# Where an output bias is added and which engine writes the normalised rows, in a two-layer attention and expert kernel

## The chip, the cores and the metric

The kernel runs on one core of a Trainium2 chip. A core has a matrix engine (TensorE, PE in the profile, with its weight loads as PEld), a vector engine (VectorE, DVE), an engine for functions of one operand (ScalarE, ACT), GpSimd (POOL), and SyncE (SP), which here issues nearly all transfers. Each takes its own instructions in order and waits for the others at semaphores. The metric is the time of one execution on the device, in microseconds (us), as the median of several runs.

## The reference

Four batches of 512 rows with 256 features pass through two layers, each an attention block and an expert block. Cut to its spine:

```python
# _layernorm(x) = (x - mean) / sqrt(var + 1e-5), row by row, without gain or shift
x = x + L0_xattn(_layernorm(x), ctx, ctx, mask)          # 16 heads, out @ Wo.T          (no output bias)
x = L0_ffn(_layernorm(x)):
    attn = attention(src) @ Wo + bo                      # src = _layernorm(x)
    y = _layer_norm(src + attn, ln1_g, ln1_b)            # with gain and shift
    y + one of 4 experts, chosen per row; _layer_norm(.., ln2_g, ln2_b)   # the result is added to x
x = x + L1_xattn(_layernorm(x), ctx, ctx, 2 * fside)     # attention(..) @ Wo.T + bo
x = x + L1_ffn(_layernorm(x))                            # 2 of 16 experts per row and 2 shared ones
```

Three attention blocks end in an output projection, two of them with a bias `bo`, and after each sum the rows are normalised for the next block. The bias, the residual and the projection are only added together, so the bias may be added to the residual at any time before.

## The kernel before, in words

All 2048 rows live in on-chip memory as 16 tiles of 128 rows by 256 features: `x` is the residual stream, `Z` the normalised rows. The program is a sequence of blocks, and all engines meet at a barrier between two blocks. Nothing is scheduled by a program: in each block every engine's instructions stand in the order in which the code of its `@block` function issues them, and a wait holds all that follows on that engine. The blocks that matter here:

- `output` (L927), called three times, for the output stages. Four rounds, one for each batch (b = 0 to 3). TensorE transposes the attention's result (L953) one round ahead of its use, ScalarE copies the turned tiles out of PSUM into `oT` (L983), TensorE multiplies them by `wo` (L967), four row tiles a round, with four PSUM tiles `py` in rotation. VectorE adds each product to the residual (L1030), takes the statistics of the row (L1001, L1038, L1040); ScalarE takes the square root (L976, one instruction of 128x4 for a round), VectorE the reciprocal (L1006), and VectorE writes the four normalised tiles (L1011; in the second call, with gain and shift, two instructions a tile, L1017 and L1021). The last three belong to `scale(b)`, which for rounds 0 to 2 stands behind the second add of the next round. Where there is a bias (second and third call) VectorE starts with four adds of 128x1024 (L995).
- ScalarE's order in `output` before: the copies of rounds 0, 1 and 2, the square root of round 0, the copies of round 3, the square roots of rounds 1 to 3. TensorE waits for both copies of a round before the matmuls of that round.
- `attention_direct` (L749), the attention of the second block, just ahead of the second output stage. VectorE takes the row minima of the scores (L897, four a head) and every fourth head divides a group of results by its sums (L520, L522).
- `queries` (L1404), ahead of the third attention. It adds the experts' output to `x` (L1539), normalises (L1542 to L1554), turns and projects the queries, and splits them into two parts: `hi` (ScalarE, L1507) and `lo` (VectorE, L1532, function `rest`). SyncE issues 2 MB of `y`, 1 MB of `common`, four transfers of 1 MB of the side input (L1436) and then the first keys (L497, L499). When the last `lo` is done GpSimd subtracts the first tile of the side input (L1464), and that ends the block.
- `attention_turned` (L525), third attention: GpSimd prepares one 128x2048 tile for each of 64 heads (L630), from a ring of four tiles that SyncE refills with 1 MB each (L588). At the 32nd head `fetch` loads `wo` and `bo` (L298, L300).

Of the kernel before, what the change touches and what calls it, by code (L numbers as in the profile page):

```python
# [19 lines left out]
ACT = mybir.ActivationFunctionType  # L20
AX = mybir.AxisListType.X

P = 128
B, S, D, H = 4, 512, 256, 16
DK = D // H
# [70 lines left out]
class Program:  # L96
# [652 lines left out]
    def attention_direct(self, QS, KS, O, fetch, ring, XS, s_qk):  # L749
# [4 lines left out]
        with ExitStack() as ctx:  # L754
# [33 lines left out]
            with nc.Block() as block:  # L788
# [99 lines left out]
                def _(eng):  # L888
                    eng.memset(pO[:], 0.0).then_inc(s_pad, 1)  # L889
                    for i in range(LAST):  # L890
# [3 lines left out]
                        for c in range(ST):  # L894
# [32 lines left out]
    def output(self, O, biased, base, dst, z, affine=None, fetch=None):  # L927


        nc, w, brow = self.nc, self.wo, self.bo  # L930
        with ExitStack() as ctx:
# [3 lines left out]
            rs = self.sb("rs", [P, NT], ctx=ctx)  # L935
            bank = self.ps("tp", [P, 4, 512], ctx)
            py = self.ps("py", [P, 4, 512], ctx)
            names = ("s_tr", "s_ev", "s_y", "s_a", "s_b", "s_st", "s_ag", "s_var", "s_dev", "s_rs", "s_g")
            s_tr, s_ev, s_y, s_a, s_b, s_st, s_ag, s_var, s_dev, s_rs, s_g = (self.sem(n, ctx) for n in names)
            with nc.Block() as block:  # L940
# [6 lines left out]
                def _(eng):  # L947
# [10 lines left out]
                    eng.wait_ge(self.s_wo, 32 if biased else 16)  # L958
# [13 lines left out]
                def _(eng):  # L972
# [4 lines left out]

                    for b in range(B):
# [5 lines left out]
                        if b >= 2:  # L984
                            deviations(b - 2)
                    deviations(B - 2)
                    deviations(B - 1)

                @block.vector
                def _(eng):  # L990
                    if biased:
                        eng.wait_ge(self.s_wo, 32)
                        for b in range(B):
                            rows = slice(b * ST, (b + 1) * ST)
                            eng.tensor_tensor(dst[:, rows, :], base[:, rows, :], brow[:].unsqueeze(1).to_broadcast([P, ST, D]),  # L995
                                              ALU.add).then_inc(s_b, 1)
                    src = dst if biased else base

# [4 lines left out]
                    def scale(b):  # L1003
# [1316 lines left out]
```

## Time and profile before

| | |
|---|---|
| three runs | 1748.32, 1748.68 and 1756.85 us, median 1748.68 us |
| the profiled execution | 1752.8 us, of it 1751.0 us span |
| busy, share of the span | PE 88%, DVE 63%, ACT 46%, POOL 26% |
| first output stage | 355 to 379 us of the span |
| `attention_direct`, second output stage | 438 to 666 us, 666 to 698 us |
| `queries`, third attention | 898 to 939 us, 939 to 1248 us |
| third output stage | 1249 to 1273 us |

An instruction is named by its line in the code, its engine and what it writes from what. A time in square brackets behind a row of the timeline is how long the engine sat idle before it and whom it waited for. TensorE's clock is given as a share of its full 2.4 GHz: 1.00 or 0.50. The chain of waits that the page prints covers only the last blocks, since every block ends in a barrier; so for each block the question is what ends it.

### The profile page before, as it was taken

To read this page: it belongs to the slowest core of one execution; us is meant where nothing else is said; L and a number is where in the kernel's file an instruction comes from. 1 tells how busy PE (TensorE), PEld (TensorE's weight loads), DVE (VectorE), ACT (ScalarE), POOL (GpSimd) and SP (SyncE) were. 2 spreads that over 40 slices of the span, in tenths; PEclk is the share of its full clock that TensorE was granted. 3 is DMA by queue.
4 is the path that set the end of the run, shared out by engine and by line. 5 is a ranking of instruction groups with operands and counts; after the bars stand their busy time and mean duration, and the time that the engine had idled before them with its cause. 6 is when DMAs were issued, how large, how long until landed. Compare 5 with 4: busy or idle time off the path is not lost. (4 is left out here: it accounts for less than half of the span.)

```text
span 1751.0 us, 24325 instructions
## 1 busy us (share of the span) xinstructions
PE 1543.9 (88%) x8312; PEld 1024.6 (59%) x8312; DVE 1108.5 (63%) x2778; ACT 812.9 (46%) x1301; POOL 455.2 (26%) x249
## 2 busy tenths in 40 slices
PE   6799999978999996699956899889888998999992
PEld 3566666655644444489944555555654556677772
DVE  6699999856887767446566888788733530122223
ACT  1388888721566672322217787777422121211110
POOL 0000000012000000301116999999122143111111
PEclk9899999999999999889978999999979999999997
DMA  7745653106343314557746988988060012144434
GB/s 252 258 153 158 180 140 85 49 13 216 92 111 104 104 43 151 198 197 248 250 183 220 313 297 300 294 290 283 4 217 0 0 49 79 56 155 157 150 111 159
DMA packets 142088, 276.68 MB, mean 158 GB/s; under 512 B 25616, under 2 KB 70160, under 8 KB 132624
## 3 DMA queue, kind: packets, MB, share of 16 engines
q1 hardware_dynamic: 134720, 258.99, 45.3%
q0 software_dynamic: 5136, 14.06, 2.2%
q10 hardware_dynamic: 2112, 2.10, 0.4%
q8 instruction: 68, 1.11, 0.3%
q14 instruction: 52, 0.43, 0.1%
HBM read 215.37 MB, written 59.69 MB: 157 GB/s over the span
## 5 line engine op out<-in xcount | busy, mean ns | idle before, releaser
L703 DVE CUSTOM_DVE_ANT_0 X<-pS,M 128x512 f32<-128x512 f32 x512 | 340.5, 689 | 54.6 <-POOL M L630 38.8
L653 PE MATMUL pT<-ident,X 128*128 128x128 f32 x2048 | 305.5, 272 | 1.7 <-ACT PT L739 1.7
L644 PE MATMUL pS<-k,q 65*128 65x512 f32 (+1 forms) x512 | 253.9, 496 | 55.0 <-DVE mx L703 35.9
L630 POOL TENSOR_TENSOR M<-C,M 128x2048 f32<-128x2048 f32 x63 | 286.0, 4603 | 6.9 <-DMA M<-in_fside_Bx16xSxS 6.5
L653 PEld LDWEIGHTS pT<-ident,X 128*128 128x128 f32 x2048 | 254.0, 140 | 41.6 <-issue 4.2
L510 PE MATMUL pO<-PT,V 128*17 128x512 f32 x1536 | 200.6, 598 | 1.0 <-ACT OT L924 1.0
L644 PEld LDWEIGHTS pS<-k,q 65*128 65x128 f32 (+1 forms) x512 | 97.9, 191 | 174.3 <-DVE mx L703 104.4
L897 DVE TENSOR_REDUCE nm<-pS 128x1 fp32r<-128x512 f32 x256 | 163.5, 684 | 40.0 <-PE pS L839 29.1
L731 ACT ACTIVATE X<-X,nm 128x512 f32<-128x512 f32 x256 | 164.0, 712 | 27.9 <-DVE nm L709 27.9
L731 ACT ACTIVATE X<-X,mx 128x512 f32<-128x512 f32 x256 | 165.2, 715 | 3.6 <-DVE mx L703 3.3
L716 DVE COPY PT<-pT 128x1024 f32<-128x1024 f32 x128 | 156.0, 1219 | 6.4 <-PE pT L653 6.4
L2040 PE MATMUL p<-xT,w 128*128 128x320 f32 x512 | 145.3, 437 | 0.5 <-ACT xT L2100 0.5
L739 ACT COPY PT<-pT 128x1024 f32<-128x1024 f32 x128 | 128.1, 1000 | 35.0 <-PE pT L653 34.0
L2126 DVE TENSOR_TENSOR g<-act,p 128x320 f32<-128x320 f32 x64 | 31.2, 487 | 166.0 <-ACT act L2089 166.0
L839 PE MATMUL pS<-rk,rq 65*128 65x512 f32 x256 | 116.4, 455 | 6.7 <-DVE pO L889 6.0
L1905 PE MATMUL p<-zT,w 128*128 128x512 f32 x256 | 122.2, 623 | 0.0
L2040 PEld LDWEIGHTS p<-xT,w 128*128 128x128 f32 x512 | 95.4, 190 | 40.4 <-issue 2.7
L2089 ACT ACTIVATE act<-p 128x320 f32<-128x320 f32 x64 | 28.0, 437 | 180.1 <-PE p L2040 180.1
L849 PE MATMUL pT<-rq,rk 97*128 97x512 f32 x256 | 102.2, 410 | 0.8 <-ACT PT L916 0.8
L839 PEld LDWEIGHTS pS<-rk,rq 65*128 65x128 f32 x256 | 48.9, 191 | 70.7 <-DVE nm L897 37.1
L916 ACT ACTIVATE PT<-pT 128x1024 f32<-128x1024 f32 x64 | 65.5, 1024 | 44.7 <-PE pT L849 44.4
L2106 POOL DMA_INDIRECT top_out<-ys,xs x32 | 30.5, 955 | 213.2 <-DVE ys L2140 211.7
(303 smaller groups left out, 2119.0 us busy)
## 6 DMA issues: line engine op xcount, KB each, us to landing
M<-in_fside_Bx16xSxS SPq DMA_DIRECT2D x64, 1024.0 KB, 7.3
w<-in_L_ffn_ew SPq DMA_DIRECT2D x48, 512.0 KB, 5.8
w<-in_L_ffn_W SPq DMA_DIRECT2D x23, 1024.0 KB, 5.4
q<-q_stacks SPq DMA_DIRECT2D x192, 64.0 KB, 3.8
M<-mask SPq DMA_DIRECT2D x16, 512.0 KB, 3.8
k<-k_stacks SPq DMA_DIRECT2D x128, 64.0 KB, 3.1
xs<-top_in SPq DMA_DIRECT2D x51, 128.5 KB, 2.2
k_stacks<-hi SPq DMA_DIRECT2D x24, 256.0 KB, 2.6
```

The lines of the kernel that those rows point to most:

```text
L510: ins = eng.matmul(pO[j * STRIP:j * STRIP + DK + 1, cols], V[:, g * GROUP + j, kt, :], PT[:, g % 2, j, kt, cols], start=(kt == 0 and cols. ...
L630: eng.tensor_tensor(M[:, slot], C[:, b % 2], M[:, slot], ALU.subtract).then_inc(s_m, 1)
L644: eng.matmul(pS[:, qt % 2, :], of, by, start=True, stop=True).then_inc(s_s, 1)
L653: ins = eng.transpose(pT[:, kt, qt * P:(qt + 1) * P], X[:, t % 3, qt, kt * P:(kt + 1) * P], self.ident[:])
L703: eng.tensor_tensor_reduce(X[:, i % 3, qt, :], pS[:, qt % 2, :], M[:, slot, qt, :], 2.0 if mask is None else 1.0, HIGHEST if mask is None ...
L716: eng.tensor_copy(PT[:, g % 2, j, 2:4, :], pT[:, 2:4, :]).then_inc(s_ed, 1)
L731: eng.activation(X[:, h % 3, qt, :], X[:, h % 3, qt, :], ACT.Exp, bias=(nm if mask is not None else mx)[:, h % 3, qt:qt + 1], scale=1.0 if ...
L739: eng.copy(PT[:, g % 2, j, 0:2, :], pT[:, 0:2, :]).then_inc(s_ea, 1)
L839: eng.matmul(bank("scores", i, qt), q[0:AUX + 1, slot, j, qt * P:(qt + 1) * P], k[0:AUX + 1, slot, j, :], start=True, stop=True).then_inc( ...
L897: eng.tensor_reduce(nm[:, pair % 2, j * ST + c:j * ST + c + 1], bank("scores", i, c), AX, ALU.min).then_inc(s_x, 1)
L1905: ins = eng.matmul(bank[:, q % 2, :], w[:, k, m * P:(m + 1) * P], zT[:, k, c * S:(c + 1) * S], start=(k == 0), stop=(k == KD - 1))
L2040: ins = eng.matmul(bank[:, m % 2, 0:CAP], w[:, i % 4, k, m * P:(m + 1) * P], xT[:, i % 2, k, :], start=(k == 0), stop=(k == KD - 1))
```

## The change

It does three things.

1. In the first and third output stage (those without gain and shift) the normalised rows are written as `x * rs + off`, with `off = -mean * rs`. VectorE computes `off` with a new instruction of 128x4 for each round, and ScalarE writes the tiles with `Identity`, with `off` as bias and `rs` as scale, both read from memory for each partition. Of the last round VectorE still writes two tiles. ScalarE now does this in `normal(b - 1)`, behind the copies of round b.
2. The bias of the second output stage is added to `Z` in `attention_direct`, one tile of 128x256 behind every third head (16 in all). The bias of the third is added to `x` in `queries`, 128x1024 for each batch, behind the first `lo` of that batch.
3. `wo` and `bo` of the third attention are loaded in `queries`, between the side input and the keys, and no longer at the 32nd head.

```diff
@@ attention_direct, VectorE, end of each of its steps
+                        n, at = divmod(i - 12, 3)
+                        if at == 0 and 0 <= n < NT:
+                            if n == 0:
+                                eng.wait_ge(self.s_wo, 32)
+                            eng.tensor_tensor(x[:, n, :], x[:, n, :], self.bo[:], ALU.add)
@@ output, ScalarE
+                    def normal(b):
+                        deviations(b)
+                        if affine is not None:
+                            return
+                        eng.wait_ge(s_off, b + 1)
+                        eng.wait_ge(s_tr, (b + 1) * KD)
+                        for n in range(b * ST, (b + 1) * ST - (2 if b == B - 1 else 0)):
+                            eng.activation(z[:, n, :], dst[:, n, :], ACT.Identity, bias=off[:, n:n + 1], scale=rs[:, n:n + 1])
+
                     for b in range(B):
                         for k in range(KD):
                             n = b * KD + k
                             eng.wait_ge(s_tr, n + 1)
                             need(eng, s_y, (b - 1) * ST)
                             eng.copy(OT[:, b % 2, k, :], bank[:, n % 4, :]).then_inc(s_ev, 1)
-                        if b >= 2:
-                            deviations(b - 2)
-                    deviations(B - 2)
-                    deviations(B - 1)
+                        if b >= 1:
+                            normal(b - 1)
+                    normal(B - 1)
@@ output, VectorE
-                    if biased:
-                        eng.wait_ge(self.s_wo, 32)
-                        for b in range(B):
-                            rows = slice(b * ST, (b + 1) * ST)
-                            eng.tensor_tensor(dst[:, rows, :], base[:, rows, :], brow[:].unsqueeze(1).to_broadcast([P, ST, D]),
-                                              ALU.add).then_inc(s_b, 1)
@@ output, VectorE, scale(b), behind the reciprocal
+                        if affine is None:
+                            eng.scalar_tensor_tensor(out=off[:, b * ST:(b + 1) * ST], in0=mv[:, b * ST:(b + 1) * ST, 0], scalar=-1.0,
+                                                     in1=rs[:, b * ST:(b + 1) * ST], op0=ALU.mult, op1=ALU.mult).then_inc(s_off, 1)
+                            if b == B - 1:
+                                eng.wait_ge(s_tr, (b + 1) * KD)
+                                for n in rows[-2:]:
+                                    eng.tensor_scalar(z[:, n, :], dst[:, n, :], mv[:, n, 0:1], rs[:, n:n + 1], ALU.subtract, ALU.mult)
+                            return
                         eng.wait_ge(s_tr, (b + 1) * KD)
-                        if affine is None:
-                            for n in rows:
-                                eng.tensor_scalar(z[:, n, :], dst[:, n, :], mv[:, n, 0:1], rs[:, n:n + 1], ALU.subtract, ALU.mult)
-                            return
@@ queries, SyncE
+                    self.load_out(eng, wo, bo)
                     for pair in range(2):
                         self.load_two_keys(eng, KS, self.k2, pair, pair, self.s_qk[pair])
@@ queries, VectorE, rest(b)
+                            if m == 0:
+                                rows = slice(b * ST, (b + 1) * ST)
+                                eng.wait_ge(s_z, (b + 1) * ST)
+                                eng.wait_ge(self.s_wo, 32)
+                                eng.tensor_tensor(x[:, rows, :], x[:, rows, :], self.bo[:].unsqueeze(1).to_broadcast([P, ST, D]), ALU.add)
```

On ScalarE, in the first output stage, the order is this before (`oT` are the turned tiles, `rs` the deviations, `Z` the normalised rows):

```order
 L745 COPY OT<-pO 128x512 x2
 L567 UNCONDITIONAL_BRANCH
-L971 UNCONDITIONAL_BRANCH
-L983 COPY oT<-tp 128x512 x6
-L976 ACT_TABLE_LOAD
-L976 ACTIVATE rs<-rs 128x4
-L983 COPY oT<-tp 128x512 x2
-L976 ACTIVATE rs<-rs 128x4 x3
-L940 UNCONDITIONAL_BRANCH
```

and this with the change:

```order
+L977 UNCONDITIONAL_BRANCH
+L998 COPY oT<-tp 128x512 x4
+L982 ACT_TABLE_LOAD
+L982 ACTIVATE rs<-rs 128x4
+L991 ACTIVATE Z<-x,off,rs 128x256 x4
+L998 COPY oT<-tp 128x512 x2
+L982 ACTIVATE rs<-rs 128x4
+L991 ACTIVATE Z<-x,off,rs 128x256 x4
+L998 COPY oT<-tp 128x512 x2
+L982 ACTIVATE rs<-rs 128x4
+L991 ACTIVATE Z<-x,off,rs 128x256 x4
```

The copies of round 2 now stand behind the deviations and the four tiles of round 0, those of round 3 behind the ones of round 1.

On VectorE, at the end of `queries`, before and then with the change (`lo` is the second part of a query tile, `x` by `bo` the moved bias):

```order
L1547 TENSOR_SCALAR rs<-mv 128x4
L1532 TENSOR_TENSOR lo<-whole,hi 128x512 x2
L1551 RECIPROCAL rs<-rs 128x4
L1554 TENSOR_SCALAR Z<-x,mv,rs 128x256 x4
L1532 TENSOR_TENSOR lo<-whole,hi 128x512 x6
```

```order
L1561 TENSOR_SCALAR rs<-mv 128x4
L1541 TENSOR_TENSOR lo<-whole,hi 128x512
L1546 TENSOR_TENSOR x<-x,bo 128x1024
L1541 TENSOR_TENSOR lo<-whole,hi 128x512
L1565 RECIPROCAL rs<-rs 128x4
L1568 TENSOR_SCALAR Z<-x,mv,rs 128x256 x4
L1541 TENSOR_TENSOR lo<-whole,hi 128x512
L1546 TENSOR_TENSOR x<-x,bo 128x1024
L1541 TENSOR_TENSOR lo<-whole,hi 128x512 x2
L1546 TENSOR_TENSOR x<-x,bo 128x1024
L1541 TENSOR_TENSOR lo<-whole,hi 128x512 x2
L1546 TENSOR_TENSOR x<-x,bo 128x1024
```

The first bias add stands ahead of the reciprocal and the normalised rows of the last batch, the last one ahead of the last `lo`.

## Rows read from the trace of the kernel before

**Rows 1.** The page's costliest groups: count, busy us and mean ns, idle before and releaser.

```profile
L630 POOL TENSOR_TENSOR M<-C,M 128x2048 f32<-128x2048 f32 x63 | 286.0, 4603 | 6.9 <-DMA M<-in_fside_Bx16xSxS 6.5
```

**Rows 2.** Timeline, VectorE, first output stage: start us, duration us, instruction, [idle before].

```profile
358.31 0.42 DVE L1030 TENSOR_TENSOR x<-x,py 128x256 f32<-128x256 f32 x1 [3.28 <-PE py L967]
...
364.18 0.16 DVE L1006 RECIPROCAL rs<-rs 128x4 f32<-128x4 f32 x1
...
375.84 0.40 DVE L1030 TENSOR_TENSOR x<-x,py 128x256 f32<-128x256 f32 x1
...
378.00 1.38 DVE L1011 TENSOR_SCALAR Z<-x,mv,rs 128x256 f32<-128x256 f32 x4
```

**Rows 3.** Timeline, ScalarE, first output stage.

```profile
361.33 1.07 ACT L983 COPY oT<-tp 128x512 f32<-128x512 f32 x2 [3.27 <-PE tp L953]
362.43 1.28 ACT L976 ACT_TABLE_LOAD   x1
```

**Rows 4.** Timeline, TensorE, first output stage and starts of the blocks behind two stages.

```profile
355.35 1.94 PE L953 MATMUL tp<-ident,Z 128*128 128x128 f32 x16 [1.08 <-PEq L567]
...
365.90 7.07 PE L967 MATMUL py<-wo,oT 128*128 128x256 f32 x32
380.54 5.87 PE L250 MATMUL pj<-ident,Z 128*128 128x128 f32 x32 [7.57 <-PEq L110]
...
1273.05 3.37 PE L250 MATMUL pt<-ident,Z 128*128 128x128 f32 x16 [6.74 <-PEq L940]
```

**Rows 5.** Timeline, VectorE, second and third output stage.

```profile
666.53 4.63 DVE L995 TENSOR_TENSOR Z<-Z,bo 128x1024 f32<-128x1024 f32 x4 [0.32 <-PEq L788]
...
675.36 0.16 DVE L1006 RECIPROCAL rs<-rs 128x4 f32<-128x4 f32 x1
...
1248.69 4.63 DVE L995 TENSOR_TENSOR x<-x,bo 128x1024 f32<-128x1024 f32 x4 [0.32 <-PEq L567]
...
1271.36 1.38 DVE L1011 TENSOR_SCALAR Z<-x,mv,rs 128x256 f32<-128x256 f32 x4
```

**Rows 6.** All groups by line: ScalarE's instructions that are nearest to the new one.

```profile
L731 ACT ACTIVATE X<-X,mx 128x512 f32<-128x512 f32 x256 | 165.2, 715 | 3.6 <-DVE mx L703 3.3
L447 ACT CAST hi<-whole 128x512 fp32r<-128x512 f32 x32 | 19.8, 618 | 67.6 <-DVE whole L427 67.6
L1642 ACT ACTIVATE sc<-tmp 128x256 f32<-128x256 f32 x1 | 0.4, 417 | 11.4 <-DVE tmp L1657 11.4
```

**Rows 7.** Timeline, end of `queries`: VectorE's `lo`, GpSimd's first tile.

```profile
920.83 1.09 DVE L1532 TENSOR_TENSOR lo<-whole,hi 128x512 fp32r<-128x512 f32 x1 [0.36 <-ACT hi L1507]
...
933.37 1.06 DVE L1532 TENSOR_TENSOR lo<-whole,hi 128x512 fp32r<-128x512 f32 x1 [0.65 <-ACT hi L1507]
934.58 4.49 POOL L1464 TENSOR_TENSOR M<-C,M 128x2048 f32<-128x2048 f32 x1 [34.86 <-DVE lo L1532]
```

**Rows 8.** Transfers issued in 902.5 to 903.3 us: KB each, us to landing.

```profile
M<-in_fside_Bx16xSxS SPq DMA_DIRECT2D x1, 1024.0 KB, 18.4
```

**Rows 9.** Timeline, VectorE, `attention_direct`, the head with a group's division.

```profile
510.07 2.57 DVE L897 TENSOR_REDUCE nm<-pS 128x1 fp32r<-128x512 f32 x4 [0.32 <-PE pS L839]
```

**Rows 10.** Timeline, SyncE and GpSimd, third attention; the last row lists transfers of 1091.56 to 1092.1 us.

```profile
1089.68 1.36 SPq L298 DMA_DIRECT2D wo<-in_L_xattn_Wo  x1
1091.08 0.47 SPq L300 DMA_DIRECT2D bo<-in_L_xattn_bo  x1
...
1102.63 4.54 POOL L630 TENSOR_TENSOR M<-C,M 128x2048 f32<-128x2048 f32 x1 [2.80 <-DMA M<-in_fside_Bx16xSxS]
...
M<-in_fside_Bx16xSxS SPq DMA_DIRECT2D x1, 1024.0 KB, 11.0
```

**Rows 11.** Windows: us, PE, PEld, DVE, ACT, POOL busy, granted clock, DMA share, GB/s.

```profile
378.00:379.00 1.00, 0.00 (x0) 0.00 (x0) 1.00 (x4) 0.00 (x0) 0.00 (x0) 0.60 0.00 0
...
385.00:386.00 1.00, 1.00 (x11) 1.00 (x10) 0.00 (x0) 0.92 (x2) 0.00 (x0) 0.99 0.00 0
...
1269.00:1270.00 1.00, 0.00 (x0) 0.00 (x0) 1.00 (x4) 0.00 (x0) 0.00 (x0) 0.54 0.00 0
...
1275.00:1276.00 1.00, 1.00 (x6) 0.86 (x6) 0.00 (x0) 0.62 (x2) 0.62 (x3) 0.55 0.63 87
```

More of the change, by code:

```diff
@@ L747, in _, with attention_direct @@
                                 eng.copy(OT[:].rearrange("c (a q) -> c a q", q=ST), pO[:].rearrange("c (q a) -> c a q", q=ST)).then_inc(s_oc, 1)
-    def attention_direct(self, QS, KS, O, fetch, ring, XS, s_qk):
+    def attention_direct(self, QS, KS, O, x, fetch, ring, XS, s_qk):
         nc = self.nc
@@ L924, in _, with output @@
                             eng.copy(OT[:], pO[:]).then_inc(s_oc, 1)
-    def output(self, O, biased, base, dst, z, affine=None, fetch=None):
-        nc, w, brow = self.nc, self.wo, self.bo
+    def output(self, O, loads, src, dst, z, affine=None, fetch=None):
+        nc, w = self.nc, self.wo
         with ExitStack() as ctx:
@@ L935, in output @@
             rs = self.sb("rs", [P, NT], ctx=ctx)
+            off = self.sb("off", [P, NT], ctx=ctx)
             bank = self.ps("tp", [P, 4, 512], ctx)
             py = self.ps("py", [P, 4, 512], ctx)
-            names = ("s_tr", "s_ev", "s_y", "s_a", "s_b", "s_st", "s_ag", "s_var", "s_dev", "s_rs", "s_g")
-            s_tr, s_ev, s_y, s_a, s_b, s_st, s_ag, s_var, s_dev, s_rs, s_g = (self.sem(n, ctx) for n in names)
+            names = ("s_tr", "s_ev", "s_y", "s_a", "s_off", "s_st", "s_ag", "s_var", "s_dev", "s_rs", "s_g")
+            s_tr, s_ev, s_y, s_a, s_off, s_st, s_ag, s_var, s_dev, s_rs, s_g = (self.sem(n, ctx) for n in names)
             with nc.Block() as block:
@@ L1026, in _ @@
                             n = b * ST + j
-                            if biased and j == 0:
-                                eng.wait_ge(s_b, b + 1)
                             eng.wait_ge(s_y, n + 1)
@@ L1402, in _, with queries @@
                             up(a, 1)
-    def queries(self, YS, x, z, zT, q_scale, QS, KS, common, side):
+    def queries(self, YS, x, z, zT, q_scale, QS, KS, common, side, wo, bo):
         nc = self.nc
@@ L2214, in build @@
             p.attention_turned(QS, KS, Z, fetch, mask=mask, ahead=(s_qk, s_f), rows=(XS2, YS2))
-            p.output(Z, False, p.x, p.x, Z, fetch=lambda eng: eng.wait_ge(p.s_w, 16 * 6))
+            p.output(Z, 1, p.x, p.x, Z, fetch=lambda eng: eng.wait_ge(p.s_w, 16 * 6))
         p.recycle()
@@ L2250, in fetch @@
                         p.load_weight(eng, n, g[("Wq", "Wk", "Wv", "bq", "bk", "bv")[n]])
-                p.attention_direct(QS, KS, O, fetch, ring, XS, s_qk)
+                p.attention_direct(QS, KS, O, Z, fetch, ring, XS, s_qk)
             with ExitStack() as inner:
@@ L2262, in fetch @@
                         p.load_second(eng, f["ln2_g"], f["ln2_b"])
-                    p.output(O, True, Z, Z, O, (grow, shift, s_affine), fetch)
+                    p.output(O, 2, Z, Z, O, (grow, shift, s_affine), fetch)
                     p.route_top1(xx, slot, tile_expert, XS, cT, KS, rw, rb, s_rw)
@@ L2273, in build @@
                 zT = p.sb("zT", [P, KD, N], ctx=inner)
-                p.queries(YS, p.x, Z, zT, -DK ** -0.5 / 2, QS, KS, common, side)
-            p.attention_turned(QS, KS, Z, lambda eng: p.load_out(eng, g["Wo"], g["bo"]), common=common, side=side)
-            p.output(Z, True, p.x, p.x, Z)
+                p.queries(YS, p.x, Z, zT, -DK ** -0.5 / 2, QS, KS, common, side, g["Wo"], g["bo"])
+            p.attention_turned(QS, KS, Z, lambda eng: None, common=common, side=side)
+            p.output(Z, 2, p.x, p.x, Z)
         middle.close()
```

3 lines of the change are left out of this document (1 added, 2 removed).

## The prediction, made before the result was known

> **What bounds the kernel now.** I read the costliest groups, then the chain of waits (it shows only the last block, because a barrier ends every block), then the timeline of each block that the edits touch, one engine at a time, and last the windows for the clock. So the question for each block is which instruction is last.
>
> The first output stage runs from TensorE's first transpose at 355.35 [rows 4] to the end of VectorE's last four tiles, 378.00 + 1.38 = 379.38 [rows 2]: 24.03 us. TensorE is done with its matmuls at 365.90 + 7.07 = 372.97 [rows 4], so from there VectorE sets the end. The third stage runs from 1248.69 to 1271.36 + 1.38 = 1272.74 [rows 5]: 24.05 us, although it has 4.63 us of bias adds at its start and the first has none. The second stage shows why: its first reciprocal stands at 675.36 - 666.53 = 8.83 us [rows 5], that of the first stage, without a bias, at 364.18 - 355.35 = 8.83 us [rows 2, 4]. VectorE would otherwise wait for the first product (3.28 us idle, [rows 2]) and for the next ones, and it has caught up before the first reciprocal. The bias adds are hidden today.
>
> In the third attention GpSimd works 286.0 us with 6.9 us idle, of which 6.5 wait for the side input [rows 1]; that chain sets its length. `queries` ends with the last `lo` at 933.37 to 934.43 and the 4.49 us of GpSimd behind it [rows 7].
>
> **The change part by part.** *Bias adds out of the output stages:* 0 in both, by the equality above.
>
> *Normalised rows on ScalarE, first stage.* Price of one `Identity` of 128x256 with two operands read for each partition: the trace has none. A 128x256 activation without such an operand is 0.417 us; a 128x512 one with one is 0.715 against 0.618 for a copy without, so one costs about 0.10 [rows 6]. Two give 0.60. Back to back, activations overlap by about 0.09 (I take it from copies: two of 0.59 take 1.07, [rows 3]), so the pitch is 0.51. From below: if the second operand is free, 0.42, and if the whole instruction goes like VectorE's tile, 1.38 for four [rows 2], about 0.33. I take 0.51, since the first operand is measured and the second is the same kind.
> The Trainium skill ("ScalarE: Activation LUTs", What ACT_TABLE_LOAD costs) says that each [128,1] pointer operand adds about 93 ns to an activation. The trace agrees for one operand (0.10 us, [rows 6]); no row has two. By its rule and its figures the pitch would be 0.49 and a stage (below) 0.2 us shorter than I put it; if the trace's 0.42 for one operand held for two, 0.8 us shorter.
>
> Now the order. The copies of round 2 stand behind the tiles of round 0, and TensorE waits for them. Reciprocal at 364.18, 0.19 on `off`, 0.17 long, so ScalarE may start at 364.58. Four tiles of 0.51 and two copies of 1.07 end at 367.70; the matmuls of round 2 start there and not at 365.90 [rows 4], 1.85 late. The next round repeats this: from the first matmul of round 2, two products of 0.86 (32 rows of the profile in 7.07 are eight products, [rows 4]), 0.31 to the add, 0.34 to the statistics, 0.34 to the reciprocal, 0.40 to the end of `off`, 2.04 of tiles, 1.07 of copies and some small lags: 6.3 us. So the matmuls of round 3 start at about 374.0 and end at 377.5, the last add starts at 377.8 (before 375.84, [rows 2]). The tail behind it was 379.38 - 375.84 = 3.54 and stays about 3.5: the square root, the reciprocal, `off` (new, 0.2), then two tiles on ScalarE (1.1) beside two on VectorE, for the four of 1.38. The stage ends at 381.3: **+1.9**. VectorE has lost 1.38 us a round, but what is late is TensorE, which waits for ScalarE. With a pitch of 0.42, nine tiles on the path cost 0.8 less: +1.0; with 0.33, +0.2. The table load is hidden before (it starts at 362.43, as soon as the copies end, [rows 3]) and after.
>
> *Third stage:* the same code and the same 24 us: **+1.9**, from +0.2.
>
> *Second stage:* ScalarE's order changes there too, but no tiles go to it. The copies of round 3 now wait for the deviations of round 1, about 14.6 us into the stage; they end at 15.9, TensorE's next product is wanted only after VectorE's 3.2 us of writing (until 18.8). **0**, at most +0.4.
>
> *Sixteen adds in `attention_direct`:* 16 x 0.42 = 6.7 us on VectorE if nothing hid them. They stand behind the last minimum of a head, where VectorE is idle until the next scores, also in the tightest head by 0.32 us [rows 9], against a pitch of about 0.33. Only four of the sixteen fall into such a head. **+0.3**, between 0 and 1.5. What is queued behind an add are the minima that free TensorE's three score banks.
>
> *Bias adds in `queries`:* 1.14 us each on VectorE (four in 4.63 less the overlap, [rows 5]). The first stands ahead of the second `lo` of batch 0, which started at 920.83 and was itself waiting 0.36 us for ScalarE [rows 7]: +0.7 for it and for the normalised rows, turning, projection and splitting of the last batch behind it. The last add stands ahead of the last `lo`, where 0.65 us was idle [rows 7]: +0.4. Together +1.1. The first add also waits for `bo`, which is now behind 4 MB of side input; the last of these was under way for 18.4 us from about 902.1 [rows 8], so it lands at 920.5, and `wo` and `bo` (0.38 MB, at the 1 MB in 3 to 4 us of that stretch) at about 921.7. The add is ready at 920.4: 1.2 us of waiting, with the reciprocal, the rows and the turning of batch 3 behind it. **+2.3**, between +1.1 (landed in time) and +4.5 (2 us later than I think). GpSimd's 4.49 us and the barrier move with it one for one.
>
> *Load taken out of the third attention:* SyncE spent 1.36 + 0.47 us and a little between on issuing `wo` and `bo`, directly ahead of a side tile, and this tile took 11.0 us to land and is the one for which GpSimd waited 2.80 us, its longest wait [rows 10]. This comes back in part: other side tiles were late without that load (6.5 - 2.80 = 3.7 us in four waits, [rows 1, 10]). **-1.5**, between -2.8 and 0.
>
> *The clock.* TensorE's clock fell to the lower level (1.2 GHz) at 378.4, 5.4 us after its last matmul of the first stage, and rose at 385.0, 4.5 us into the next block [rows 4, 11]. In the third stage it fell at 1269.5, 3.2 us after the last matmul, and rose at 1275.95 [rows 11]. TensorE's pause ahead of the next block is 7.57 and 6.74 us [rows 4]; it now works until 4.5 us later and the next block starts 1.9 later, so the pauses are 5.0 and 4.1 us, among the times in which it fell. Where it stays up, the transposes of the next block go at ScalarE's pace of about 0.5 us a copy: I put 2.0 and 1.3 us on that (of 6.6 and 6.7 us). Half of it: **-1.6**, between -3.3 and 0.
>
> **Sum:** 1.9 + 1.9 + 0 + 0.3 + 2.3 - 1.5 - 1.6 = **+3.3 us**. On the profiled execution that is 1752.8 + 3.3 = 1756.1; this execution took 4.1 us more than the median of the runs, so in their terms 1748.7 + 3.3 = **1752.0 us**. That is 0.2%. About 0.5%, or 8.7 us, is what a measurement of this kernel can tell from no change, so the likeliest verdict is "no difference".
>
> **The rivals.**
> *A. ScalarE is cheap.* Tiles at 0.33 to 0.42. For: VectorE writes such a tile in that time. Against: every ScalarE row with an operand for each partition is dearer. The stages cost +0.2 to +1.0 each and not +1.9, the sum is -0.1 to +1.5: 1749.4.
> *B. VectorE's end decides.* The copies are not held up, and the stages end earlier by what VectorE loses. For: TensorE is done 6.4 us before the stage ends. Against: the order on ScalarE, and a round trip of 6.3 us a round. If it held, the last add would start 0.3 behind TensorE's end of 372.97 and not at 375.84, 2.5 us earlier, of which the new `off` takes 0.2: 2 x -2.3, with +0.3, +2.3, -1.5 and the clock at -1.3 it is -4.8: 1743.9.
> *C. The bias arrives late and stops `queries` (slower).* One mechanism: the add of batch 0 waits at the head of VectorE's queue. If `bo` lands after 925 and not at 921.7, the last batch is 4 us later, TensorE has a pause of over 5 us at 923, the clock falls as it did at 378.4, and 7 us of query matmuls take up to 12: +2.3 + 3.3 + 5, with the rest +1.0: +11.6, 1760.3. It decides from a landing at about 925. For: 7 MB are ahead of it in that stretch. Against: the last side tile is in at 920.5 [rows 8], and `wo` and `bo` are small beside it.
> *D. The load did nothing to GpSimd, and the clock falls as before:* 3.3 + 1.5 + 1.6 = +6.4, 1755.1.
>
> **How the numbers follow.** Forecast (net +1.5 to +5) 0.45, A 0.20, B 0.08, C 0.10, D 0.17. The range of the forecast with its own bounds is 1748 to 1755; to hold 8 of 10 it must take in A and D whole and leave out half of B and most of C, with 2 us for the spread of the runs: **1744.5 to 1758**. Faster by over 0.5% (below 1740.0) needs B with every other term at its lower end: 0.05. Slower by over 0.5% (above 1757.4) is C and a small part of D: 0.12. Same: 0.83.
>
> **What would show it.** In the first and third stage ScalarE's copies of rounds 2 and 3 start only behind four `Identity` rows each, of about 0.60 us, TensorE's matmuls of round 2 start 12.4 us into the stage (before 10.55) and the stages last 25.9 us. The second stage still lasts 31.6 us. In `queries` the first add of 128x1024 has an idle time before it that a DMA ends, and GpSimd's first tile starts 2.3 us later from the block's start. GpSimd's wait of 2.80 us in the middle of the third attention is gone or smaller. I am wrong if the stages are shorter than 24.0 us, if the add in `queries` waits over 4 us, or if the third attention changes in length by more than 3 us.

## The result, and the profile after

The changed kernel took 1762.31 us (median of 14 runs, 1758.68 to 1767.68), the kernel before 1756.51 us on the same chip (14 runs, 1748.32 to 1765.50). The ratio is 1.0037, with a 95% interval of 1.0019 to 1.0055: 3.3 to 9.7 us slower. The forecast was +3.3 us and 1752.0; the time lies outside the range of 1744.5 to 1758.

The first view is the page of the changed kernel: its span, and GpSimd's row in the third attention (answers to [rows 1]).

```profile
span 1761.7 us, 24341 instructions
...
L630 POOL TENSOR_TENSOR M<-C,M 128x2048 f32<-128x2048 f32 x63 | 286.0, 4595 | 3.4 <-DMA M<-in_fside_Bx16xSxS 3.0
```

GpSimd now waits 3.0 us for the side input and not 6.5. The next view is TensorE's timeline in the first output stage, from the transposes of round 3 on, which it does ahead of the matmuls of round 2 (columns as in [rows 4]).

```profile
364.86 1.04 PE L959 MATMUL tp<-ident,Z 128*128 128x128 f32 x8
367.48 3.72 PE L973 MATMUL py<-wo,oT 128*128 128x256 f32 x16 [1.58 <-ACT oT L998]
373.65 5.41 PE L973 MATMUL py<-wo,oT 128*128 128x256 f32 x16 [2.46 <-ACT oT L998]
383.72 6.11 PE L250 MATMUL pj<-ident,Z 128*128 128x128 f32 x32 [4.66 <-PEq L110]
```

Where [rows 4] had one run of 32 records without a pause, TensorE now waits twice for ScalarE's copies of `oT`, 1.58 and 2.46 us. The stage began at 355.18, so the matmuls of rounds 2 and 3 start 12.30 and 18.47 us into it. The second thing to see is the length: 16 records take 3.72 us in round 2 and 5.41 in round 3. ScalarE in the same stretch (answers to [rows 3]):

```profile
364.40 2.08 ACT L991 ACTIVATE Z<-x,off,rs 128x256 f32<-128x256 f32 x4 [1.72 <-DVE off L1015]
366.38 1.04 ACT L998 COPY oT<-tp 128x512 f32<-128x512 f32 x2
367.32 0.21 ACT L982 ACTIVATE rs<-rs 128x4 f32<-128x4 f32 x1
...
381.48 1.09 ACT L991 ACTIVATE Z<-x,off,rs 128x256 f32<-128x256 f32 x2 [0.44 <-DVE off L1015]
```

The copies stand behind the four tiles, as the order says. The windows (columns as in [rows 11]; the last but two is the granted clock) show why round 3 is slow, first stage and then third:

```profile
375.00:376.00 1.00, 1.00 (x5) 0.79 (x4) 0.25 (x1) 0.00 (x0) 0.00 (x0) 0.52 0.00 0
376.00:377.00 1.00, 1.00 (x4) 0.81 (x3) 0.83 (x3) 0.00 (x0) 0.00 (x0) 0.50 0.00 0
377.00:378.00 1.00, 1.00 (x3) 0.76 (x3) 0.30 (x2) 0.79 (x2) 0.00 (x0) 0.50 0.00 0
1270.00:1271.00 1.00, 1.00 (x4) 0.82 (x3) 0.00 (x0) 0.00 (x0) 0.00 (x0) 0.50 0.00 0
1271.00:1272.00 1.00, 1.00 (x4) 0.82 (x3) 0.42 (x1) 0.00 (x0) 0.00 (x0) 0.50 0.00 0
```

The clock is at 1.2 GHz while TensorE is busy in the middle of the stage. The third stage repeats the first:

```profile
1263.23 3.72 PE L973 MATMUL py<-wo,oT 128*128 128x256 f32 x16 [1.58 <-ACT oT L998]
1269.40 5.36 PE L973 MATMUL py<-wo,oT 128*128 128x256 f32 x16 [2.45 <-ACT oT L998]
1278.57 1.06 PE L250 MATMUL pt<-ident,Z 128*128 128x128 f32 x8 [3.81 <-PEq L946]
```

In `queries` (answers to [rows 7]) VectorE's first and last rows of the new work, and GpSimd behind them:

```profile
925.00 1.23 DVE L1546 TENSOR_TENSOR x<-x,bo 128x1024 f32<-128x1024 f32 x1 [0.34 <-DMA bo<-in_L_xattn_bo]
...
939.12 1.05 DVE L1541 TENSOR_TENSOR lo<-whole,hi 128x512 fp32r<-128x512 f32 x1
```

```profile
940.32 4.49 POOL L1473 TENSOR_TENSOR M<-C,M 128x2048 f32<-128x2048 f32 x1 [36.43 <-DVE lo L1541]
945.15 9.07 POOL L630 TENSOR_TENSOR M<-C,M 128x2048 f32<-128x2048 f32 x2 [0.34 <-POOLq L1437]
```

Every block begins at a barrier, so a block's length is one difference of two starts, and an output stage repeats to 0.03 us where neither its order nor its clock changes (24.35 to 24.38, 22.36 and 22.37). This is the measure I use below. "Stage + pause" runs from TensorE's first transpose to its first of the next block; "queries" from GpSimd's first memset to its first tile of L630; "rest" is all behind the third stage, whose code no kernel here touches. Microseconds:

| profile | stage 1 + pause | attention 2 | queries | attention 3 | stage 3 + pause | rest |
|---|---|---|---|---|---|---|
| before | 25.19 | 285.99 | 41.64 | 309.28 | 24.36 | 477.95 |
| changed | 28.54 | 286.24 | 43.22 | 305.78 | 27.64 | 483.13 |
| changed, again | 28.54 | 285.66 | 43.15 | 306.38 | 29.22 * | 472.63 |
| copies first | 22.37 | 289.67 | 43.50 | 304.96 | 21.51 | 468.13 |
| ScalarE rows only | 30.09 * | 285.83 | 42.06 | 308.94 | 26.01 | 479.89 |
| bias and load only | 26.76 * | 285.90 | 43.48 | 304.40 | 24.35 | 473.36 |
| load only | 25.20 | 290.22 | 41.72 | 306.33 | 24.38 | 472.81 |
| pauses filled | 29.20 | 285.19 | 43.49 | 307.52 | 28.34 | 471.90 |
| pauses filled, shorter | 26.85 | 286.65 | 43.30 | 306.18 | 26.00 | 479.77 |
| one operand | 22.19 | 289.77 | 43.23 | 305.59 | 22.88 * | 472.68 |
| best version | 22.36 | 284.88 | 41.60 | 306.71 | 21.52 | 468.08 |
| best, other chip | 22.36 | 285.16 | 41.97 | 307.60 | 21.52 | 471.67 |
| best, end filled | 22.36 | 293.46 | 41.84 | 307.37 | 21.51 | 477.98 |
| end filled, other chip | 23.90 * | 289.29 | 41.64 | 308.02 | 23.07 * | 468.92 |

A star marks a stage whose first 16 transposes took 2.8 to 3.6 us and not 1.94: the clock was already down as the stage began, worth 1.4 to 1.6 us.

Between before and changed the five touched blocks of the table add 3.35 + 0.25 + 1.58 - 3.50 + 3.28 = 4.96 us, in line with the 5.8 us of the medians. The sixth, the second output stage, is as long as before (32.00 us with its pause, against 32.01). The rest adds 5.18 in this pair of profiles and is 5.32 below the kernel before in the other profile of the changed kernel, so it is scatter.

### The profile page after: what moved, and what is told of

The parts are those of the page before. It is cut to its first block and busy times, and to the rows that moved or that the text cites. A ratio compares the mean times of both kernels' runs of the same rounds, so it can differ in the third digit from the quotient of the medians.

```text
span 1761.7 us, 24341 instructions
## 1 busy us (share of the span) xinstructions
PE 1554.2 (88%) x8312; PEld 1031.3 (59%) x8312; DVE 1103.2 (63%) x2770; ACT 826.5 (47%) x1329; POOL 455.5 (26%) x249
## 5 line engine op out<-in xcount | busy, mean ns | idle before, releaser
L630 POOL TENSOR_TENSOR M<-C,M 128x2048 f32<-128x2048 f32 x63 | 286.0, 4595 | 3.4 <-DMA M<-in_fside_Bx16xSxS 3.0
```

The costliest lines, as they stand in the source:

```text
L630: eng.tensor_tensor(M[:, slot], C[:, b % 2], M[:, slot], ALU.subtract).then_inc(s_m, 1)
```

## The experiments

The theory (T1): the order on ScalarE holds TensorE up, and in the pauses so made its clock comes down. Against it: writing on ScalarE is dear in any order (T2), or the difference is clock scatter in blocks that nobody touched (T3).

**Copies first.** The changed kernel with one edit on ScalarE.

```diff
-                        if b >= 1:
-                            normal(b - 1)
+                        if b >= 2:
+                            normal(b - 2)
+                    normal(B - 2)
                     normal(B - 1)
```

> The changed kernel, but ScalarE does its copies of a round ahead of the normalised rows of two rounds before, as the kernel before did. T1 (the order on ScalarE holds TensorE up, and the clock falls in the pauses this makes): TensorE is not held, the matmuls of round 2 start 10.5 us into the first and third output stage (12.3 in the changed kernel), the clock stays at 1.00 to the end of round 3, and the stage lasts about 21.5 us instead of 27.4, so each of the two stages is 6 us shorter than in the changed kernel. T2 (the writing on ScalarE and the round trip for the offset make the stage longer in any order): still 26 us or more. T3 (the stages cost nothing that lasts, the difference of the medians is the clock in untouched blocks): the total is as that of the changed kernel. By T1 the total is 10 to 12 us below the changed kernel, about 5 below the kernel before; queries +1.6 us and the third attention -3.5 us against before as in the changed kernel.

Measured: 1742.46 us against 1751.13 (12 and 35 runs), ratio 0.9958 (0.9931 to 0.9985). ScalarE and TensorE in the first stage, which begins at 357.89:

```profile
363.88 1.07 ACT L998 COPY oT<-tp 128x512 f32<-128x512 f32 x2 [3.27 <-PE tp L959]
...
367.11 2.08 ACT L991 ACTIVATE Z<-x,off,rs 128x256 f32<-128x256 f32 x4 [0.64 <-DVE off L1016]
...
378.02 1.09 ACT L991 ACTIVATE Z<-x,off,rs 128x256 f32<-128x256 f32 x2 [0.44 <-DVE off L1016]
```

```profile
368.45 7.07 PE L973 MATMUL py<-wo,oT 128*128 128x256 f32 x32
380.26 5.22 PE L250 MATMUL pj<-ident,Z 128*128 128x128 f32 x32 [4.74 <-PEq L110]
```

TensorE's pauses inside the stage are gone, the matmuls of round 2 start 10.56 us into the stage, all 32 records take 7.07 us again. Without the pause behind it the stage lasts 21.2 us, 2.8 less than before the change and 6.2 less than after it. The tiles still cost 2.08 us for four; they are only off the path. T2 has fallen, and so has T3: stage by stage the lengths follow the order and not the run.

**ScalarE rows only.** The kernel before, with `normal` in the new order, and neither bias nor load moved (the edit on ScalarE; `normal`, `off` and VectorE's part are those of the change).

```diff
-                        if b >= 2:
-                            deviations(b - 2)
-                    deviations(B - 2)
-                    deviations(B - 1)
+                        if b >= 1:
+                            normal(b - 1)
+                    normal(B - 1)
```

> The kernel before with one part of the change: ScalarE writes the normalised rows in its new order; the bias adds stay at the start of the output stages and the load of Wo and bo in the third attention. T1: the first and third stage last 27.4 us each (24.0 before), queries stays at 41.6 us and the third attention at 309.3; in the third stage the bias adds are still hidden. If the bias adds ahead of the third stage were worth something there, the third stage is longer than the first by up to 4.6 us. Total +6.7 us against before. T3: total as before.

Measured: 1758.86 us (12 runs), ratio 1.0031 (1.0006 to 1.0056). The first stage shows the changed kernel's rows, 3.72 and 5.41 us in rounds 2 and 3. The third differs, and its rows tell most in this study:

```profile
1266.40 3.72 PE L969 MATMUL py<-wo,oT 128*128 128x256 f32 x16 [1.58 <-ACT oT L994]
1272.58 3.72 PE L969 MATMUL py<-wo,oT 128*128 128x256 f32 x16 [2.46 <-ACT oT L994]
1280.11 1.06 PE L250 MATMUL pt<-ident,Z 128*128 128x128 f32 x8 [3.81 <-PEq L942]
```

```profile
1274.00:1275.00 1.00, 1.00 (x6) 0.90 (x5) 0.63 (x3) 0.00 (x0) 0.00 (x0) 1.00 0.00 0
```

The same two pauses, and here the clock stayed at 1.00. The stage with its pause takes 26.01 us against 24.36 before: the order alone costs 1.65 us, and the clock, where it falls, 1.6 to 1.7 more. My expectation of 27.4 us for a stage held for the first only, whose 30.09 us with the pause hold a slow start worth 1.55. The bias adds at the start of the third stage cost nothing, as in the kernel before.

**Bias and load only.** The changed kernel with VectorE writing the rows and ScalarE's old order (VectorE's edit, cut; on ScalarE only the square roots are left, placed as in the kernel before).

```diff
-                            if b == B - 1:
-                                eng.wait_ge(s_tr, (b + 1) * KD)
-                                for n in rows[-2:]:
+                            for n in rows:
                                     eng.tensor_scalar(z[:, n, :], dst[:, n, :], mv[:, n, 0:1], rs[:, n:n + 1], ALU.subtract, ALU.mult)
```

> The changed kernel with the normalised rows on VectorE and ScalarE's order as before: only the bias adds and the load of Wo and bo are moved. T1: the first and third stage last 24.0 us each, with the clock at 1.00 to the end of round 3; queries +1.6 us, the first attention +0.2, the third attention -3.5, so the total is 1 to 2 us below before. If the bias adds in the third stage had been on the path, that stage is shorter than 24 by up to 4.6 us. Rival on the third attention: its -3.5 us is scatter in the landing of the side tiles, and it lasts about 309 us here.

Measured: 1747.97 us, ratio 0.9999 (0.9974 to 1.0024). The third stage is 24.35 us, the first 26.76 with a slow start; the matmuls of rounds 2 and 3 take 7.07 in both. The total of 1 to 2 us below the kernel before that I expected can't be told from none by this ratio. Taking the bias adds out of the third stage is worth nothing, and `queries` pays 1.8 us for it here.

**Load only.** The kernel before, with the load of Wo and bo issued in `queries`.

```diff
                     for n in range(4):
                         eng.dma_start(self.M[:, n], side[n]).then_inc(self.s_f[n], 16)
+                    self.load_out(eng, wo, bo)
```

> The kernel before with one edit: the load of Wo and bo for the third output stage is issued in queries, behind the four side tiles, and no longer in the third attention. If the load is the cause of the 3.5 us, the third attention lasts 305.8 us and GpSimd's waits for DMAs in it fall from 6.5 to about 3.0 us; queries stays at 41.6 us if its +1.6 came from the adds alone, and is up to 0.5 longer if the load delays the side tiles or the keys. If the 3.5 us are scatter, the third attention lasts about 309 us. Output stages 24.0 us each by every theory.

Measured: 1750.68 us, ratio 0.9990 (0.9966 to 1.0014). GpSimd's row of this kernel, and of "ScalarE rows only", where the load stays in the attention:

```profile
L630 POOL TENSOR_TENSOR M<-C,M 128x2048 f32<-128x2048 f32 x63 | 286.1, 4584 | 3.8 <-DMA M<-in_fside_Bx16xSxS 3.5
```

```profile
L630 POOL TENSOR_TENSOR M<-C,M 128x2048 f32<-128x2048 f32 x63 | 286.0, 4578 | 6.6 <-DMA M<-in_fside_Bx16xSxS 6.2
```

The third attention lasts 309.28 and 308.94 us in the two profiles with the load, and 304.40 to 308.02 in the twelve without it, 306.4 on average: 2.7 us for the load, with scatter of 2 us to each side. The waits of GpSimd for the side input, in the same row, are 6.5 and 6.2 us with the load and 1.7 to 5.3 in the twelve. Neither the lengths nor the waits of the two groups overlap, and this run differs from the kernel before in the load alone, so the load is the cause; its size rests on two profiles, and the ratio above holds -2.7 us (0.15%) as well as zero. `queries` lasts 41.60 to 42.06 us in seven profiles without the adds, whether the load is in it or not, and 43.15 to 43.50 in seven with them: the adds cost 1.6 us on average, the load at most some tenths.

**Pauses filled.** The changed kernel, with matmuls whose product nobody reads in the two pauses.

```diff
+                        if affine is None and b >= 2:
+                            need(eng, s_a, b * ST - 3)
+                            for _ in range(6 if b == 2 else 10):
+                                eng.matmul(py[:, 0, 0:D], self.ident[:], w[:, 0, :], start=True, stop=True)
                         eng.wait_ge(s_ev, (b + 1) * KD)
```

> The changed kernel with 6 and 10 more matmuls of 128x256 (their products are thrown away) in the first and third output stage, in TensorE's pauses ahead of the matmuls of rounds 2 and 3 (1.6 and 2.5 us, 0.23 us a matmul). If the clock falls inside the stage because TensorE pauses there, it stays at 1.00 to the end of round 3 in both stages, the 16 matmuls of round 3 take 3.7 us and not 5.4, and each stage lasts 25.7 us and not 27.4. If the clock falls there for another reason (its phase from the attention before), at least one of the two stages still shows 5.4 us. The matmuls of round 2 still start 12.3 us into the stage by every theory, since the copies stand behind the tiles.

Measured: 1755.96 us against 1745.25, ratio 1.0065 (1.0044 to 1.0086). I had taken one record for one matmul; the trace has two for each:

```profile
365.35 2.76 PE L971 MATMUL py<-wo,ident 128*128 128x256 f32 x12
...
371.39 4.48 PE L971 MATMUL py<-wo,ident 128*128 128x256 f32 x20
375.71 3.62 PE L977 MATMUL py<-wo,oT 128*128 128x256 f32 x16
```

Round 3 takes 3.62 us at full clock in both stages, but the fill outlasts the pauses and holds the real matmuls back: those of round 2 start 13.15 us into the stage and not 12.3. It was run again with 3 and 5 matmuls in place of 6 and 10.

> As the run with the filled pauses, in which 6 and 10 matmuls took 2.76 and 4.48 us (0.45 us each and not 0.23) and so outlasted the pauses they were to fill. Now 3 and 5 matmuls, 1.4 and 2.2 us in pauses of 1.6 and 2.5. If the pauses bring the clock down: the matmuls of round 2 start 12.3 us into the stage as in the changed kernel, round 3's take 3.7 us at a clock of 1.00 in both stages, and a stage with the pause behind it lasts 26.9 us (first) and 25.9 (third) instead of 28.5 and 27.6; total about 3 us below the changed kernel. If it falls for another reason, one of the stages has its 5.4 us again.

Measured: 1760.98 us against 1758.83, ratio 1.0013 (0.9988 to 1.0038). The first stage, and a window in round 3 of the third stage (the first has the same):

```profile
367.59 3.72 PE L977 MATMUL py<-wo,oT 128*128 128x256 f32 x16 [0.28 <-ACT oT L1002]
371.14 2.32 PE L971 MATMUL py<-wo,ident 128*128 128x256 f32 x10
373.77 3.72 PE L977 MATMUL py<-wo,oT 128*128 128x256 f32 x16 [0.30 <-ACT oT L1002]
382.14 6.53 PE L250 MATMUL pj<-ident,Z 128*128 128x128 f32 x32 [4.66 <-PEq L110]
```

```profile
1271.00:1272.00 1.00, 1.00 (x7) 0.87 (x6) 0.97 (x5) 0.10 (x1) 0.00 (x0) 1.00 0.00 0
```

The copies still end late, the rounds start where they did in the changed kernel, and the stages with their pause last 26.85 and 26.00 us, as expected to 0.1: +1.66 and +1.64 against before. The total was to be some 3 us below the changed kernel; 1.0013 beside the changed kernel's 1.0037 fits that, but the intervals overlap. So the two parts of a stage's 3.3 us are apart: 1.65 us is the order, 1.6 to 1.7 us the clock. Over all profiles, six stages had the pauses unfilled and the clock fell in five; four had them filled and it fell in none; eighteen had none, and rounds 2 and 3 took 7.07 us in each.

**One operand.** "Copies first", with `scale=0.5` in place of `scale=rs[:, n:n + 1]`. It leaves out the scaling by row, so only its durations are of use; it was run once.

> The version with the copies first, and with a constant as the scale of the normalised rows on ScalarE (they lack the scaling by row, so later values are others): each tile reads one operand for each partition and not two. Four tiles take 2.08 us with two operands. If each operand costs what the first one does in the kernel before (0.10 us), four take about 1.75 us, one about 0.50; if the second operand was free, they still take 2.08.

Measured, ScalarE in the first stage:

```profile
364.38 1.71 ACT L991 ACTIVATE Z<-x,off 128x256 f32<-128x256 f32 x4 [0.64 <-DVE off L1016]
```

Four tiles take 1.71 us and not 2.08, two take 0.91 and not 1.09. So the pitch of a tile is 0.40 and 0.495 us: the second operand costs 0.09 us, as much as the first [rows 6]. Rival A's cheap tile does not exist. The Trainium skill ("ScalarE: Activation LUTs", What ACT_TABLE_LOAD costs) gives about 93 ns to each such operand, and by this run the trace agrees for the second too.

**The changed kernel again.**

> The changed kernel once more, for the scatter of its blocks. What the order on ScalarE causes must repeat to 0.1 us: matmuls of rounds 2 and 3 behind idle times of 1.58 and 2.46 us in both stages, queries 43.2 to 43.5 us, the third attention 305 to 306 us. What the clock does may differ: round 3's matmuls take 3.7 or 5.4 us, the first attention lasts 286 or 290 us, and the part behind the third stage 478 to 483 us.

Measured: what the order causes repeats to 0.01 us (28.54, pauses of 1.58 and 2.45), and what the clock and the DMAs do varies, the rest by 10.5 us (472.63, below the 478 to 483 that I expected). Round 3 took 5.41 us in both stages.

**The best version.** The kernel before, with ScalarE writing the rows behind the copies, and the load in `queries`; the biases stay where they were (cut).

```diff
+                    self.load_out(eng, wo, bo)
...
                         if b >= 2:
-                            deviations(b - 2)
-                    deviations(B - 2)
-                    deviations(B - 1)
+                            normal(b - 2)
+                    normal(B - 2)
+                    normal(B - 1)
```

> A version made of what the runs so far pay for: the kernel before, with ScalarE writing the normalised rows of the first and third stage behind the copies of two rounds later, and with the load of Wo and bo issued in queries behind the side tiles; the bias adds stay at the start of the output stages. T1: the first and third stage with the pause behind them last 22.4 and 21.5 us (25.2 and 24.4 before), queries 41.7 us (the adds in it cost 1.6), the first attention as before, the third attention about 305.5 us. Total -2.8 - 2.9 - 3.5 = about 9 us below before, and 1 to 2 us below the version with the biases moved. If VectorE, freed of the tiles but with 4.6 us of bias adds ahead of the third stage, does not catch up before the end of round 3, the third stage lasts up to 2 us longer than the first.

Measured: 1734.61 us against 1745.25 (6 and 17 runs), ratio 0.9932 (0.9905 to 0.9959); on another chip 1746.78 against 1749.91, ratio 0.9972 (0.9949 to 0.9995). In the profiles -2.83 and -2.84 us in the stages and -2.6 or -1.7 in the third attention. VectorE catches up with its 4.6 us of bias adds even without a tile to write:

```profile
368.11 7.07 PE L969 MATMUL py<-wo,oT 128*128 128x256 f32 x32
379.91 5.35 PE L250 MATMUL pj<-ident,Z 128*128 128x128 f32 x32 [4.74 <-PEq L110]
...
1252.86 7.07 PE L969 MATMUL py<-wo,oT 128*128 128x256 f32 x32
```

By the ratios it beats both kernels; by how much, 3 or 11 us of the medians, the two chips leave open.

> The version made of what paid, once more, on one chip with the variant that fills the pause behind the stages. Its blocks should repeat: first and third stage with their pause 22.4 and 21.5 us, queries 41.7, the third attention 305 to 307. Ratio to the kernel before 0.993 to 0.996.

Measured: the blocks repeat as expected (22.36 and 21.52 us, `queries` 41.97, the third attention 307.60). The ratio of 0.9972 lies above the expected 0.993 to 0.996, into which its interval reaches.

**The pause behind the stage filled.** The best version with seven matmuls behind TensorE's last.

```diff
+                    if affine is None:
+                        eng.wait_ge(s_a, NT - 3)
+                        for _ in range(7):
+                            eng.matmul(py[:, 0, 0:D], self.ident[:], w[:, 0, :], start=True, stop=True)
```

> The version made of what paid, with 7 more matmuls (3.1 us, products thrown away) behind TensorE's last product of the first and third stage, where it pauses for 4.7 and 3.9 us before the next block and where the clock came down at 380.0 and 1264.4 as the next block began. If that pause brings the clock down, the clock is at 1.00 at the start of the next block and its first 32 transposes take about 4.3 us and not 5.35 and 6.1, which is 1 and 1.5 us less a block, 1732 us in all against 1734.6 there. If the clock falls for another reason, nothing changes. The stages themselves keep their 21.5 us.

Measured: 1751.39 us against 1758.83 (12 and 23 runs), ratio 0.9954 (0.9929 to 0.9979). The next block's transposes, and the windows of the whole second attention, of this kernel and of the one without the fill:

```profile
377.89 3.68 PE L250 MATMUL pj<-ident,Z 128*128 128x128 f32 x32 [1.70 <-PEq L110]
```

```profile
377.89:671.35 293.46, 281.06 (x1328) 148.46 (x1329) 203.90 (x338) 160.21 (x201) 17.38 (x5) 0.95 0.36 102
```

```profile
379.91:664.79 284.88, 272.46 (x1328) 144.10 (x1329) 202.50 (x337) 160.33 (x201) 17.38 (x5) 0.98 0.37 105
```

32 transposes take 3.68 us and not 5.35, a better start than the 4.3 I had expected. The attention behind them then ran at a mean clock of 0.95 and not 0.98 and lasted 8.6 us longer. A single profile can't tell whether that is the fill's doing, so both were run on one chip.

> The variant with 7 matmuls in the pause behind the first and third stage, on the same chip. The clock is again at 1.00 at the start of the next block, whose first 32 transposes take 3.7 us and not 5.35. If this gain lasts, its ratio to the kernel before is 0.002 below that of the version without; if the clock comes down later instead (in the profile of this variant the first attention lasted 293.5 us and not 285), it is the same or above.

Measured: 1746.54 us with the fill and 1746.78 without, ratios 0.9965 (0.9935 to 0.9994) and 0.9972 (0.9949 to 0.9995). The attention lasted 289.3 us with the fill, 285.2 without. The gain behind the first stage was 1.7 us in both profiles, and behind the third the 32 transposes took 5.1 us and not 6.0 to 6.1; neither reaches the total. That the fill itself brings the clock down later is not shown, since it also fell in that attention in "copies first", "load only" and "one operand" (289.7 to 290.2 us at a mean clock of 0.96 and 0.97).

## Why the prediction was right and wrong

The time was 10.3 us above the forecast: 7.8 us of that lie in the time of the kernel before that it was built on, 2.5 in the difference (+5.8 measured, +3.3 said). Of the difference the mechanism was the forecast's. The copies of round 2 stand behind four tiles, TensorE starts at 12.30 us (said: 12.4), four tiles take 2.08 us (said: 2.04), the table load is hidden, the second stage is as before (32.00 us against 32.01). By its own steps:

| term | said | measured |
|---|---|---|
| first and third stage, order | +1.9 each | +1.65 each |
| clock | -1.6 | none behind the stages, +1.7 inside each |
| adds in `attention_direct` | +0.3 (0 to 1.5) | +0.3 and -0.3 in two profiles |
| `queries` | +2.3 (1.1 to 4.5) | +1.6 |
| load out of the third attention | -1.5 (-2.8 to 0) | -2.7 |

**In the difference, the step that failed is the clock's.** I wrote that the shorter pause behind the stage (now 4.66 and 3.81 us) would sometimes leave the clock up, "half of it: -1.6". It did so in no way that helped: the transposes of the next block took 6.11 us after 5.87. The clock did come down later than before (381.9 and not 378.2), but it also came back later, at 388.7 and not 385.0, and so fell on the transposes all the same:

```profile
381.00:382.00 1.00, 0.00 (x0) 0.00 (x0) 0.89 (x4) 0.56 (x3) 0.00 (x0) 0.93 0.03 8
...
388.00:389.00 1.00, 1.00 (x8) 1.00 (x7) 0.00 (x0) 0.59 (x2) 0.00 (x0) 0.65 0.00 0
```

The forecast also read [rows 11] a little late: 0.60 and 0.54, as means of 1.00 and 0.50 over a microsecond, put the falls at 378.2 and 1269.1, not 378.4 and 1269.5, which is 5.2 and 2.8 us behind the last matmul. I did not ask what the two new pauses inside the stage would do, though the walk gave both, the start of round 2 at 367.70 and of round 3 at 374.0. With them the clock came down to 1.2 GHz under round 3, +1.7 us a stage where -0.8 was said. Two stages make 3.4 + 1.6 = 5.0 us of error in this term.

**The other terms erred the other way.** The order was 0.5 us too dear over the two stages. In `queries` the first add waited 0.34 us and not 1.2: it was ready 22.7 us into the block, as said, but `bo` was in at 23.1 us and not at 23.9. The third attention gained 1.2 us more than said, and GpSimd's wait of 2.80 us in its middle is gone (the three left are of 1.19, 1.05 and 0.78 us); in the first profile it changed by 3.50 us, which is over the 3 us that the forecast had set as a sign of being wrong, in the second by 2.90. Measured with these terms the sum is 3.3 + 3.4 + 1.6 - 2.7 = 5.6 us, beside 5.8 of the medians.

**The larger part of the miss was the base.** The forecast put +3.3 us on 1748.68, a median of three runs. The kernel before has a median of 1756.51 in the 14 runs whose first three these are, and 1745.25 to 1758.83 on the other chips. With the right difference on that base the answer would have been 1754.5, inside the range; with the forecast's difference on 1756.51 it would have been 1759.8, outside. The step that failed here is the term of "2 us for the spread of the runs" in the range: the 14 runs spread over 17 us. Two of the three lay within 0.4 us, the third was 8 us off, and the median of the 14 lies beside that one; three runs could not tell.

**The rivals.** A fell by the price of the operand. B did not happen, because the copies are held up, but it named what the better order gives: it put such a stage at 24.03 - 2.3 = 21.7 us, and "copies first" has 21.2. C's late bias was 0.34 us. D came nearest with +6.4, by two errors that cancel: it gave nothing for the load, which paid 2.7 us, and nothing for the clock, which cost 3.4. "Same" as the likeliest verdict holds by its bound of 0.5%, below which the interval of 0.19% to 0.55% almost all lies; but the interval leaves out zero, and the changed kernel is slower.

## What to carry to other kernels

When work moves to an engine that others wait for, put it behind what they wait for: the same tiles cost 1.65 us a stage ahead of the copies and gain 2.8 behind them. Price a wait on TensorE twice, once for its length and once for the clock under the matmuls that follow: here 1.65 and 1.7 us, the second in five stages of six. Compare blocks between barriers, which repeat to 0.03 us in the output stages, before whole runs, which here scatter by 17 us on one chip; and take more than three runs for the base.

## What the runs showed of the hardware

- The clock came down while TensorE worked. In the changed kernel it was idle for 1.58 us, busy for 3.7, idle for 2.46, and 1.4 us into the next matmuls of the first stage the clock was at 1.2 GHz; in the third stage it got there as they began (1269.3). In one stage of six the same pattern left it at 2.4 GHz, so the pattern alone doesn't decide it.
- Holding the clock up in one place did not shorten the kernel (1746.54 and 1746.78 us). In the profiles TensorE's mean granted clock over the whole span was 0.950 and 0.955 of full speed with the end filled, 0.960 and 0.961 without; over all twelve runs of each on one chip it was 0.956 with and 0.955 without, so the fill shows no effect on it.
- From run to run the time goes with that mean clock. Of the 35 runs of the kernel before on one chip, the five at 0.949 to 0.951 took 1756.68 to 1764.30 us and the ten at 0.957 to 0.960 took 1741.05 to 1749.20. Time and clock go together here; what sets a run's mean clock is not shown.
- ScalarE stood still for some us behind the third stage with its input ready, in untouched code. In the changed kernel:

```profile
1474.49 0.70 ACT L1936 COPY common<-py 128x256 f32<-128x256 f32 x2 [4.69 <-remote]
```

```profile
1469.43 0.38 PE L1903 MATMUL py<-w,g 128*128 128x256 f32 x1 [0.24 <-issue]
1474.91 1.65 PE L1903 MATMUL py<-w,g 128*128 128x256 f32 x3 [5.11 <-ACT common L1936]
```

The product that the copy reads was there at 1469.81, and nothing that the profile shows ended the wait. TensorE's idle time at this line was 6.0 us in the kernel before, 5.9 here, and none in the second profile of the changed kernel and in the first of the best version. The four profiles with 5.9 to 6.3 us of it have a rest of 478 to 483 us, the seven without any one of 468 to 473, so it goes with most of that scatter. Its cause stays open.
